# A first router worked out group by group inside the retention, shared ups in halves, two shared downs ahead of the routed blocks

## The reference

```
h = h + retention(layernorm(h))
t = layernorm(h)
hs = gelu(einsum('td,nfd->ntf', t, sw1) + sb1)          # 2 shared experts, 512 hidden units
shared = einsum('ntf,ndf->td', hs, sw2) + sb2.sum(0)
probs = softmax(t @ gate_w.T + gate_b)                  # 8 routed experts
top_v, top_i = top_k(probs, 2)
routed = sum over the two chosen experts of top_v * expert(t)
h = h + shared + routed
```

## Time and profile before

| | us |
|---|---|
| median of 3 runs (199.64 to 200.83) | 200.12 |
| the profiled execution | 201.99 |
| its span | 199.8 |
| PE busy in the span | 169.2 |
| DVE busy | 98.1 |
| ACT busy | 76.5 |
| POOL busy | 76.1 |

### The profile page before, as it was taken

How to read it: one execution, slowest core, us unless ns; L and a number is a source line. 1 busy time by engine, 2 the same in 40 slices (tenths; PEclk the granted TensorE clock), 3 DMA queues, 4 the chain that set the end, 5 groups by cost and what they waited for, 6 DMA issues and landing times.

```text
span 199.8 us, 3828 instructions
## 1 busy us (share of the span) xinstructions
PE 169.2 (85%) x1342; PEld 128.8 (64%) x1345; DVE 98.1 (49%) x373; ACT 76.5 (38%) x230; POOL 76.1 (38%) x98
## 2 busy tenths in 40 slices
PE   6798999978998999999999989998997999767100
PEld 2775567866774899999869467548874457545000
DVE  0054669786390226885212933784676623422104
ACT  2036616442527246565720175447424005323100
POOL 8500335004782017887430320001367605557500
PEclk9999999995559699999999999999999999999555
DMA  6979999990111319993112019995011162111142
GB/s 211 261 215 316 379 283 386 411 385 34 48 44 35 90 32 294 343 322 113 39 53 88 24 43 311 438 277 123 3 46 30 43 139 46 34 34 46 38 122 57
DMA packets 18924, 31.18 MB, mean 156 GB/s; under 512 B 4793, under 2 KB 12470, under 8 KB 18522
## 3 DMA queue, kind: packets, MB, share of 16 engines
q1 hardware_dynamic: 15552, 27.15, 41.7%
q0 software_dynamic: 2752, 3.37, 6.5%
q10 hardware_dynamic: 602, 0.42, 0.7%
HBM read 23.58 MB, written 7.40 MB: 155 GB/s over the span
## 4 chain that ended last, share of the span: by engine, by line
PE 64%; DMA 9%; issue 6%; DVE 6%; ACT 5%; POOL 5%; SPq 2%; another core or an unknown queue 1%; POOLq 1%; ACTq 0%; DVEq 0%
PE ps L1378 60%; POOL rooms L550 4%; DMA w_proj<-in_w_proj 4%; PE ps L1845 1%; DMA rooms<-xm,room 1%; DMA o_tok<-o_rows 1%; SPq L415 1%; DMA o_rows<-o_sb,result_row 1%; DMA xb<-rooms 1%; PE ps L1629 1%; ACT ln_std L619 1%; DVE o_sb L1349 1%; ACT L818 1%; POOLq L82 1%
## 5 line engine op out<-in xcount | busy, mean ns | idle before, releaser
L557 POOL DMA_INDIRECT o_rows<-o_sb,result_row x16 | 21.0, 1310 | 19.6 <-DVE o_sb L1121 17.1
L760 ACT ACTIVATE hid_b<-ps,w_ring 128x128 f32<-128x128 f32 x64 | 18.2, 368 | 16.2 <-PE ps L1378 15.4
L596 POOL DMA_INDIRECT o_rows<-o_sb,result_row x16 | 15.0, 940 | 16.7 <-DVE o_sb L1349 12.9
L1378 PE MATMUL ps<-xbT,w_ring 128*128 128x128 f32 x128 | 17.8, 284 | 0.0
L528 POOL TENSOR_TENSOR ln_rstd<-ln_var,minus_half 119x1 f32<-119x1 f32 x7 | 4.0, 569 | 35.9 <-DVE ln_var L895 35.9
L550 POOL DMA_INDIRECT rooms<-xm,room x10 | 11.4, 1145 | 15.5 <-issue 15.5
L1378 PE MATMUL ps<-w_ring,hid_b 128*128 128x128 f32 x128 | 17.0, 276 | 0.3 <-ACT hid_b L760 0.3
L1378 PEld LDWEIGHTS ps<-xbT,w_ring 128*128 128x128 f32 x128 | 16.4, 200 | 0.0
L1378 PE MATMUL ps<-filler 128*128 128x512 bf16 x56 | 15.0, 406 | 1.6 <-DVE filler L904 1.5
L859 ACT ACTIVATE hid<-ps,moe_b 128x64 f32<-128x64 f32 x32 | 8.3, 310 | 21.2 <-PE ps L1378 12.5
L1378 PEld LDWEIGHTS ps<-w_ring,hid_b 128*128 128x128 f32 x128 | 15.6, 192 | 0.5 <-ACT hid_b L760 0.5
(11 more groups left out here) (211 smaller groups left out, 343.2 us busy)
## 6 DMA issues: line engine op xcount, KB each, us to landing
w_ring<-in_w_routed SPq DMA_DIRECT2D x16, 514.0 KB
m<-in_m SPq DMA_DIRECT2D x2, 2048.0 KB, 12.3
rooms<-zeros SPq DMA_DIRECT2D x8, 330.0 KB, 5.4
patchesT<-in_patchesT SPq DMA_DIRECT2D x6, 272.0 KB, 6.1
xb<-rooms SPq DMA_DIRECT2D x16, 66.0 KB
w_s<-in_w_s SPq DMA_DIRECT2D x2, 512.0 KB, 5.6
moe_b<-in_moe_b SPq DMA_DIRECT2D x2, 512.0 KB, 17.8
rooms<-zeros SPq DMA_DIRECT2D x1, 792.0 KB, 8.2
```

The lines of the kernel that those rows point to most:

```text
L557: nc.gpsimd.indirect_dma_start(o_rows[:], bass.IndirectOffsetOnAxis(ap=result_row[:, b:b + 1], axis=0), o_sb[:, b, :], None).then_inc(o_sc ...
L596: nc.gpsimd.indirect_dma_start(o_rows[:], bass.IndirectOffsetOnAxis(ap=result_row2[0:past_, j:j + 1], axis=0), o2_sb[0:past_, j, :], None) ...
L760: nc.scalar.activation(hid_b[:, b % RING, c, :], ps[:, b % 2, c * BS:(c + 1) * BS], ACT.Gelu, bias=w_ring[:, b % WRING, FF + c:FF + c + 1] ...
L1378: return nc.tensor.matmul(out_, lhsT, rhs, start=first, stop=last)
```

## The change

Six edits, all between the embedding and layer 1:

1. *Opening.* `values_gates(0)` and the first half unit stand between the turns of xn; the score units' halves are single (`unit(u, a)`); DVE instead of ACT copies `w_score`; two of the four pairs of filler products go. ACT loads the tables of Silu and Sqrt by explicit small activations, gates 1 to 4 directly behind their values.
2. *Order of the retention.* `turn_z` is split (`turn_bias` earlier), and group 0's and 1's output, turn and logits stand ahead of the last groups' retains and centres; DVE and ACT have new lists, with `decayed(3)` and `decayed(4)` cut into parts.
3. *Router by group.* `mark`, `rooms_of` and `place` work on one group at a time; the logits' bias is a product of its own (`logit_bias`); `scatter(g)` waits for `g + 1` rooms.
4. *Trial scatter.* POOL first writes 16 rows of zeros to a spare place and waits for it.
5. *Shared ups in halves.* 16 half units with three banks in turn; the first three stand among the last groups' routers, and seven stand between group 4's logits and its rooms.
6. *Downs.* EARLY = 3: two behind the ups, ahead of the block turns, the third behind the first block's ups, two behind all blocks.

The diff, cut to its core; of the written-out lists a few lines stand:

```diff
-SHARED_BANKS = (6, 7, 2, 3, 6)
-EARLY = 1
+SHARED_BANKS = (6, 7, 6, 2, 3)
+EARLY = 3
+UP_BANKS = (3, 4, 5)
...
-                pool.wait_ge(room_ready, (1, 3, 3, 5, 5)[g])
+                pool.wait_ge(room_ready, g + 1)
...
+            nc.gpsimd.indirect_dma_start(
+                rooms[:], bass.IndirectOffsetOnAxis(ap=spare_row[0:16, 5:6], axis=0),
+                zeros[0:16, 0:RW], None).then_inc(rooms_tried, 16)
+            pool.wait_ge(rooms_tried, 16)
...
+            def hidden_out(half, e, c):
+
+                own = slice(half * HALF, (half + 1) * HALF)
+                nth = half * NS * FC + e * FC + c
+                act.wait_ge(up_done, nth + 1)
+                nc.scalar.activation(hid_s[:, e, c, own], ps[:, UP_BANKS[nth % len(UP_BANKS)], 0:HALF], ACT.Gelu,
+                                     bias=b1_cols[:, e * FC + c:e * FC + c + 1]).then_inc(hid_ready, 1)
+
+            values_out0(0)
+            act.wait_ge(proj_done, 1)
+            nc.scalar.copy(halves(qT0[:, 0, :]), ps[:, 0:2, 0:HALF]).then_inc(proj_out, 1)
...
+            nc.scalar.activation(warm[:], eps_col[0:1, 0:1], ACT.Silu)
+            gate_out0(0)
+            for g in range(1, G):
+                values_out0(g)
+                gate_out0(g)
+            nc.scalar.activation(warm[:], eps_col[0:1, 0:1], ACT.Sqrt)
             heads_out(0)
...
             dve.wait_ge(tables_ready, 1)
             here(dve, "b2_all")
+            shared_joined(0)
+            shared_joined(1)
             turned_out(0)
...
+            def unit(u, a):
+
+                pe.wait_ge(score_out, u + 1)
+                pe.wait_ge(xT_ready, G if a else 3)
+                last = mm(ps[:, 2 * u + a, 0:HALF], w_score[:, u, :], xT[:, a * HALF:(a + 1) * HALF])
+                if a:
+                    last.then_inc(proj_done, 1)
+
+            turn_tokens(0, (0,))
+            fill(2, 0)
+            turn_tokens(0, (1,))
+            fill(2, 0)
+            turn_tokens(0, (2,))
+            values_gates(0)
+            turn_tokens(0, (3,))
+            unit(0, 0)
+            turn_tokens(0, (4,))
+            unit(0, 1)
+            unit(1, 0)
+            unit(1, 1)
...
+            def rooms_of(g):
+
+
+                n = rows(g)
+                dst = ps[0:n, g % 2, GT + ER:GT + 2 * ER]
+                pe.wait_ge(picks_ready, g + 1)
+                mm(dst, ones[0:1, 0:n], room_base[:, 0:ER], True, False)
+                for f in range(g):
+                    mm(dst, ones[:, 0:n], either[:, f, :], False, False)
+                pe.wait_ge(first2_ready, g + 1)
+                mm(dst, before[0:n, 0:n], either[0:n, g, :], False, True).then_inc(room_done, 1)
...
+            def shared_up(half, e, c):
+
+                nth = half * NS * FC + e * FC + c
+                if nth == 0:
+                    pe.wait_ge(s_out, 4 * G)
+                elif nth == 1:
+                    pe.wait_ge(yT_out, G)
+                elif nth == 2:
+                    pe.wait_ge(yc_gated, G)
+                else:
+                    pe.wait_ge(hid_ready, nth - 2)
+                pe.wait_ge(xT_ready, 2 * G if half else G + 3)
+                mm(ps[:, UP_BANKS[nth % len(UP_BANKS)], 0:HALF], w1_s[:, e, c * 128:(c + 1) * 128],
+                   xT[:, half * HALF:(half + 1) * HALF]).then_inc(up_done, 1)
...
+            shared_up(0, 0, 0)
             retention_out(4)
+            shared_up(0, 0, 1)
+            logit_bias(3)
             turn_x(3)
+            rooms_of(2)
             first_logits(3)
+            shared_up(0, 0, 2)
             turn_x(4)
+            rooms_of(3)
+            logit_bias(4)
             first_logits(4)
+            shared_up(0, 0, 3)
+            for c in range(FC):
+                shared_up(0, 1, c)
+            shared_up(1, 0, 0)
+            shared_up(1, 0, 1)
+            rooms_of(4)
+            counts()
+            for c in range(2, NS * FC):
+                shared_up(1, c // FC, c % FC)
...
+            shared_down(0)
+            shared_down(1)
+            pe.wait_ge(hid_ready, 2 * NS * FC)
             pe.wait_ge(tables_ready, 1)
             turn_block(0)
             turn_block(1)
             turn_block(2)
             block_ups(0)
-            for g in range(EARLY):
-                shared_down(g)
+            shared_down(2)
```

More of the change, by code:

```diff
@@ L749, in _ @@
-            here(act, "b1_cols")
+            hidden_out(0, 0, 1)
+            hidden_out(0, 0, 2)
+            hidden_out(0, 0, 3)
+            for c in range(FC):
+                hidden_out(0, 1, c)
             for e in range(NS):
                 for c in range(FC):
-                    act.wait_ge(up_done, e * FC + (c + 1))
-                    nc.scalar.activation(halves(hid_s[:, e, c]), ps[:, 2 * (c % 2):2 * (c % 2) + 2, 0:HALF],
-                                         ACT.Gelu, bias=b1_cols[:, e * FC + c:e * FC + c + 1]).then_inc(hid_ready, 1)
+                    hidden_out(1, e, c)
@@ L949, in decayed @@
                     dve.wait_ge(y_done, g - 1)
-                for r in range(4):
+                for r in parts:
                     dve.wait_ge(s_done, 4 * g + r + 1)
@@ L1041, in _ @@
+            scale_heads(1)
             scale_heads(2)
-            aggregate(1, 0)
+            decayed(4, (2, 3))
             head_var(3)
+            scale_heads(3)
             retained(1)
+            pick(0)
             stats(1, 1)
-            root_inverse(0)
-            scale_heads(3)
-            normalised(0)
+            mark(0)
             aggregate(1, 1)
             head_var(4)
+            root_inverse(1)
+            place(0)
+            normalised(1)
             retained(2)
@@ L1052, in _ @@
             stats(1, 2)
-            root_inverse(1)
             scale_heads(4)
-            normalised(1)
             aggregate(1, 2)
+            pick(1)
+            root_inverse(2)
+            normalised(2)
+            mark(1)
             retained(3)
             stats(1, 3)
-            root_inverse(2)
-            pick(0)
-            mark(0, 1)
-            normalised(2)
+            place(1)
             aggregate(1, 3)
+            pick(2)
+            root_inverse(3)
+            mark(2)
@@ L1064, in _ @@
+            normalised(3)
             retained(4)
             stats(1, 4)
-            place(0, 1)
-            root_inverse(3)
-            pick(1)
-            normalised(3)
             aggregate(1, 4)
-            pick(2)
-            mark(1, 2)
+            place(2)
             root_inverse(4)
             normalised(4)
-            place(1, 2)
             pick(3)
+            mark(3)
+            place(3)
             pick(4)
-            mark(3, 2)
-            place(3, 2)
+            mark(4)
@@ L1378, in mm, with turn @@
                 return nc.tensor.matmul(out_, lhsT, rhs, start=first, stop=last)
-            def turn(ready, base, src, turned, evacuated, after=False, bank=5, banks=2, groups=range(G), between=None,
-                     fill_bank=None):
+            def turn(ready, base, src, turned, evacuated, after=False, bank=5, banks=2, groups=range(G), between=None):
                 for g in groups:
@@ L1569, in _ @@
             scores(3)
+            centre(1)
             retain(2)
-            centre(1)
-            scores(4)
-            retain(3)
             turn_z(0)
```

258 lines of the change are left out of this document (124 added, 134 removed).

## The result

The changed kernel took 199.46 us in the median of 22 runs (196.65 to 204.02), the kernel before, run beside it, 201.1. The ratio of the two is **0.987, with a 95% interval of 0.984 to 0.990**: 2.6 us less at 200 us, where 2.9 was forecast. Executions of one and the same kernel differ in time and in their mean granted clock (0.899 to 0.939 for the changed kernel), and every ratio here compares only those within 1.5% of the fastest of their kernel, 12 of these 22; the medians of all 22, 199.46 and 201.1, would give 0.992. The profiled execution took 198.62 (span 196.7, mean clock 0.933), against 201.99.

The account below looks back on a forecast made before the run. The chain of waits was taken to run through PE and, from 47 to 60 us, POOL's ten scatters, the two nearly level before the blocks. The terms -1.0 - 1.9 = -2.9 took the median from 200.12 to 197.2, range 193.8 to 200.8.

Parts of the forecast that it names:

- Behind the blocks: After the blocks, two downs fewer; the first expert join, bound by its DMA, starts at 107.3: -1.9, bounds 0 and 3.6.
- Ahead of the blocks: Up to the block turns and ups: the second block's ups start at 69.5 instead of 70.47, -1.0.
- the clock's low stretch: PE's clock before the blocks: low as before, back at 56.6 (56.0 to 57.3) during the seven half ups.
- Opening: Start of the retention: scores of group 0 at about 20.6 instead of 21.10, 0.5 on the chain, 1.25 of PE work.
- The Sqrt load: On ACT, 1.28 ahead of the first head copy, which comes 0.3 later at 27.9; taken as nothing.
- First scatter: On POOL, at about 42 rather than 47.28, 0.3 after its rooms, with 1.1 as the bound.
- Groups 0 to 3 at POOL's pace by 55: On POOL, their scatters follow at pace by about 55, then a gap of some 4 us before the ninth.
- Group 4's logits: On PE in the router, end at 52.9 against 50.98 before, bounds 51.2 and 55.4.
- The tenth scatter: Last scatter on POOL, at 60.85 against 60.37, held by the last group's rooms.
- Scatter beside the long subtraction: POOL's ninth scatter beside DVE's subtraction on the weights: up to 0.48 may be added, taken as 0.
- Rival "high clock": PE before the blocks: clock high throughout, -4.3 - 1.9 = -6.2, 193.9; chance 0.12.
- Rival "slower": Router: five PE-ACT-DVE round trips delay group 4's logits; at 5.5 us late (58.4), +2.6, 202.7; chance 0.13.

Follow-up runs that it names:

- e1: The changed kernel with the downs as before (EARLY = 1, the two early downs back behind all blocks); ratio to the kernel before 1.0145.
- e11: The kernel before with twelve filler products in PE's waits between group 0's turn and group 3's logits; ratio to the kernel before 1.0175.
- e5: The changed kernel itself, run again beside other kernels; ratio to the kernel before 0.9826, 195.16 us.
- e4: The changed kernel without the trial scatter; ratio to the kernel before 0.9883, from two of its four executions.
- e9: The changed kernel with thirteen filler products in PE's waits and the opening's last turn ahead of the first score half; ratio to the kernel before 0.9713.
- e7: The changed kernel with ten filler products in PE's waits between group 0's rooms and group 2's logits; ratio to the kernel before 0.9673.
- e2: The kernel before with only the changed kernel's order of downs and joins (EARLY = 3); ratio to the kernel before 1.0016.
- e3: The changed kernel with group 4's rooms and the counts behind two half ups instead of seven; ratio to the kernel before 0.9949.
- e8: The changed kernel with the opening's last turn of xn ahead of the first score half; ratio to the kernel before 0.9818, from three of eight executions.

## Why the prediction was right

Its two terms, -1.0 ahead of the blocks and -1.9 behind, stand differently. That the ratio's 2.6 us is so near to 2.9 is in part luck: in the first pair of traces one term was 1.0 too large and the other 0.4 too small, and how much the first one gives depends on where the clock falls. By the medians of all executions the gain is 1.6.

- **Behind the blocks: right.** Keys minus b is 45.1 in each trace with four late downs (before, e1, e11) and 42.3 to 43.0 in each with two. That is -2.3 in the first pair; the join waits for its DMA, which landed 106.8 and not 107.3. The term was 0.4 too small.
- **Ahead of the blocks: right mechanism, a size that the forecast could not fix.** b - a is -0.04 in the first trace and -1.48 in e5, both against one trace of the kernel before. The forecast took the place of the clock's low stretch as fixed; it is not. Given its place, the steps held: the clock came back at 57.8, 3.6 after ups ran back to back (54.18), where 3.7 was taken, no idle over 0.5 stood before the turns, and first ups and third down ran at the high level.
- **Opening: mis-sized.** 0.5 was taken for scores of group 0, 0.07 came, or 0.27 if one counts from the first turn of xn (14.21 before, 14.41 now), whose start differs from execution to execution. The last halves start at 18.51 and not at 18.09: they wait for ACT's copy of group 4, behind its turn. The Sqrt load (27.05, 1.28, the small activation following at 28.35) put the first head copy at 28.46 and not at 27.9; PE's first centre product came no later for it (29.89, before 30.23). The Trainium skill, "ScalarE: Activation LUTs", "What ACT_TABLE_LOAD costs", would have the switch with its drain twice as long; this trace again shows the row's 1.28, with the next activation at once.
- **First scatter: mis-sized.** The 0.3 for a waiting scatter was wrong for the first one, where the bound 1.1 was right (1.01), trial or not (e4). It was right for the ninth (rooms at 60.19, scatter at 60.49).
- **Groups 0 to 3 at POOL's pace by 55: wrong.** POOL waited for group 1's and group 2's rooms as well, and the eighth scatter started at 56.26. It cost nothing, since the ninth waits for group 4.
- **Group 4's logits: 54.34** instead of 52.9, within the bounds. 0.4 of it is the opening. The walk over PE's order gave 32.3 from scores to logits; 33.3 came in the first trace and 32.0 in e5, so the other 1.0 goes with the earlier fall and not with the walk. The tenth scatter stood at 61.91 instead of 60.85: the rooms came 0.4 sooner behind the logits than worked out.
- **Scatter beside the long subtraction:** taken as 0; the tenth began first (61.91, 62.57) and ran 1.10.
- **Rival "high clock"** did not occur by itself. Its price agrees with what fillers made of it: b - a of e9 is 4.4 below before, where 4.3 was forecast ahead of the blocks; e7's better executions are 3.3% below before, 6.5 us, for a forecast of 6.2.
- **Rival "slower"** did not come: group 4's logits would have had to end past 57.
- What the prediction did not see is how much the two parts need each other: it gave each its own sum, and e1 and e2 show that neither stands alone.

## What to carry to other kernels

When two engines are level ahead of a barrier, moving one of them earlier makes an idle stretch, and the gain is what is put into that stretch: undo each half of such a change and expect the pieces not to add up. Price work by the clock at which it will run, and ask of every gap on PE whether the low level follows it; a few filler products in the gaps around the first fall were worth about as much here as the reordering itself (ratio 0.983 to 0.971 or 0.967, the change 1 to 0.983), but only where nothing else was next in line. And look at more than one execution: one profile may hold the usual case or not.

## What the runs showed of the hardware

- **The point of the fall varies from execution to execution.** In two traces of one program the clock fell at 44.1 and 46.6 (changed), 23.1 and 25.0 behind the first scores; in e3, e4, e7 and e8, whose order of work is the same from the scores to that point, it fell at 40.1 to 41.3, 18.7 to 19.1 behind them. It came back between 54 and 64. Executions of e5 with a mean clock of 0.932 to 0.942 took 194.2 to 195.4, those at 0.916 and 0.921 took 199.1 and 197.7. The Trainium skill, "TensorE: Matmul & The Clock Gate", section "What's actually happening", says that the clock follows how busy PE has been recently, in a reckoning that runs on by itself and does not restart with the kernel; a fall that moves while the work does not agrees with it.
- **Filling the gaps held the clock.** Three fillers in a gap of 0.7 at 37 and ten up to 47 went with no fall at all before the last slices in the profiled execution of e9, and with a mean clock of 0.955 or more in all six, for 13 x 0.22 = 2.9 us of PE work, part of it in waits.
- **PE's wait of 3.8 to 3.9 us was followed by a second fall** of three to four microseconds (e1, e11), which came 0.9 to 1.4 behind the end of the wait and cost 1.6 to 1.7 us on the ups and the down. In the kernel before, a wait of 1.2 was followed by one as well (66.0 to 69.4); waits of 0.3 and 0.4 at the same place in the changed kernel, e5 and e9 were not.
- **The first scatter, after POOL had idled 12 to 14 us,** starts 1.0 to 1.1 behind its rooms (before, changed, e4), and a trial transfer well ahead of it changes 0.1. Later ones that had waited 1.0 to 3.2 us for rooms started 0.3 behind them (changed).
